# A decoder layer on one core: the chunk tails in seven steps fewer, with the knots counted at once and the picks transposed a step sooner

## What is computed

```python
x = x + attn(layernorm(x))            # softmax over 1024 keys, 16 heads
x = x + xattn(layernorm(x), ctx, mask)
# routed part, on xf = layernorm(x):
def _calibrate(scores, knots, temperature):        # 8 knots
    idx_float = sigmoid(scores / (temperature[0] + 1e-6)) * (K - 1)
    idx_low = clip(int(idx_float), 0, K - 2)
    t = idx_float - idx_low
    return knots[idx_low] + t * (knots[idx_low + 1] - knots[idx_low])
cluster_idx = argmax(_calibrate(xf @ cluster_sigs.T))     # 8 clusters
local_idx = argmax(_calibrate(xf @ sigs.T)[of that cluster])  # 8 tiles in each
comp = tanh(gelu(xf @ w1 + b1) @ w2 + b2)
mag = relu(comp . spline_w1[tile] + b) . spline_w2[tile] + b
y = xf + mag * directions[tile] * output_scale
x = x + layernorm(y) * gamma + beta
```

## Time and profile before

| | us |
|---|---|
| median of 3 runs | 1819.47 |
| lowest, highest | 1817.64, 1820.15 |
| the profiled execution's own time | 1818.39 |
| its span, first to last instruction | 1816.1 |
| PE busy | 1727.1 |
| DVE busy | 1163.6 |
| ACT busy | 1143.8 |
| POOL busy | 892.8 |

### The profile page before, as it was taken

One profiled execution on the slowest core, in us unless ns is written; L12 is line 12 of the kernel. 1 busy time (PEld: TensorE's weight loads), 2 busy tenths in 40 slices (PEclk: granted clock), 3 DMA queues, 4 the chain that ended last, 5 costly groups with the idle time before them and its releaser, 6 DMA issues.

```text
span 1816.1 us, 27480 instructions
## 1 busy us (share of the span) xinstructions
PE 1727.1 (95%) x9160; PEld 831.3 (46%) x9160; DVE 1163.6 (64%) x2784; ACT 1143.8 (63%) x1554; POOL 892.8 (49%) x811
## 2 busy tenths in 40 slices
PE   6999999999999899999999999999999999999994
PEld 4444454454544344454444435445454444544352
DVE  6575538567476765747657576665756767385767
ACT  5577756666476765666566764676656677567652
POOL 2444454645544544546645364545645456444620
PEclk9999999999999999999999999999999999999997
DMA  4300000101200000010200000001020001000000
GB/s 146 74 13 1 1 13 1 36 1 24 48 1 13 1 24 1 1 36 1 58 13 1 13 1 24 1 1 36 1 59 1 2 1 24 13 1 1 1 12 12
DMA packets 97246, 32.39 MB, mean 18 GB/s; under 512 B 76753, under 2 KB 91217, under 8 KB 97105
## 3 DMA queue, kind: packets, MB, share of 16 engines
q1 hardware_dynamic: 97104, 30.64, 8.1%
HBM read 13.56 MB, written 4.19 MB: 10 GB/s over the span
## 4 chain that ended last, share of the span: by engine, by line
PE 79%; ACT 8%; DVE 7%; issue 4%; POOL 1%; DMA 0%; ACTq 0%; DVEq 0%; SPq 0%; POOLq 0%
PE attended L1387 22%; PE key_scores L1366 21%; PE misc L1295 7%; PE misc L1427 6%; PE max_scores L1344 6%; PE misc L1467 3%; PE misc L1397 3%; ACT relu L1770 2%; ACT probs L1779 2%; PE misc L1458 2%; PE misc L1531 1%; PE misc L1300 1%; DVE relu L2073 1%; PE misc L1520 1%; PE misc L1509 1%
## 5 line engine op out<-in xcount | busy, mean ns | idle before, releaser
L1779 ACT ACTIVATE probs<-key_scores 128x1024 f32<-128x1024 f32 x512 | 524.6, 1025 | 455.9 <-PE key_scores L1366 392.7
L2581 POOL TENSOR_TENSOR prob_sum<-prob_sum,probs 128x512 f32<-128x512 f32 x383 | 492.2, 1285 | 133.0 <-ACT probs L1779 108.8
L1387 PE MATMUL attended<-probs,values 128*64 128x512 f32 x2048 | 551.4, 617 | 0.1
L2073 DVE CUSTOM_DVE_ANT_0 relu<-max_scores,relu 128x512 f32<-128x512 f32 x508 | 330.2, 687 | 248.5 <-PE max_scores L1344 247.1
L1366 PE MATMUL key_scores<-q_high,k_chain 64*128 64x512 f32 x2048 | 457.9, 443 | 19.0 <-ACT probs L1779 17.5
L1366 PEld LDWEIGHTS key_scores<-q_high,k_chain 64*128 64x128 f32 x2048 | 191.6, 184 | 459.2 <-ACT probs L1779 226.8
L2095 DVE TENSOR_TENSOR running_sum<-running_sum,probs 128x512 f32<-128x512 f32 x384 | 266.3, 694 | 11.4 <-ACT probs L1779 4.3
L1770 ACT ACTIVATE relu<-max_scores 128x1024 f32<-128x1024 f32 x254 | 259.1, 1020 | 13.5 <-PE max_scores L1344 10.8
L2577 POOL TENSOR_TENSOR prob_sum<-probs 128x512 f32<-128x512 f32 x64 | 82.1, 1283 | 349.2 <-PE misc L1397 342.3
L1344 PE MATMUL max_scores<-k_max,q_high 64*128 64x512 f32 x1016 | 209.6, 408 | 11.9 <-DVE row_max L2073 10.7
L1366 PE MATMUL key_scores<-q_low,k_chain 64*128 64x512 f32 x1024 | 202.9, 392 | 0.0
(11 more groups left out here) (457 smaller groups left out, 1897.4 us busy)
## 6 DMA issues: line engine op xcount, KB each, us to landing
k_chain<-k_chain SPq DMA_DIRECT2D x32, 256.0 KB, 3.7
shift_row<-row_max SPq DMA_DIRECT2D x512, 0.5 KB, 2.0
buf_a<-in_x SPq DMA_DIRECT2D x8, 512.0 KB, 4.0
x_in<-in_x SPq DMA_DIRECT2D x7, 512.0 KB, 4.8
k_max<-k_max SPq DMA_DIRECT2D x14, 256.0 KB, 3.5
out_x<-buf_b SPq DMA_DIRECT2D x7, 512.0 KB, 3.2
heads_out<-in_qkv_wT SPq DMA_DIRECT2D x1, 1536.0 KB, 10.0
wo<-in_o_wT SPq DMA_DIRECT2D x1, 1024.0 KB, 6.3
```

Of the source, the lines that this page charges most:

```text
L1387: tensor.matmul(attended[head * HD:(head + 1) * HD, :], values_of(b, g // 2)[:, kt, g % 2 * HD:(g % 2 + 1) * HD], prob_slot(u, kt, head), ...
L1779: scalar.activation(probs[(u * KT + kt) % len(probs)][:, :, :], key_scores[:, :, :], ACT.Exp).then_inc(S["exp"])
L2073: vector.tensor_tensor_reduce(out=relu_of(u, i)[:, head, :], in0=max_area(u, i)[:, head, :], in1=relu_of(u, i)[:, head, :], scale=1.0, sca ...
L2581: gpsimd.tensor_tensor(prob_sum[1][:, :], prob_sum[1][:, :], probabilities, ALU.add).then_inc(S["prob_sum1"])
```

## The change

In `calibration` one yield goes: `cal_d` and `cal_e` now stand in the same step as `cal_b`. In `tail` one yield before `pickT` goes, so that the transposition is put in the step after `pick_one`; `mag` loses its own step and is put in the same step as the first `y`; the second `gamma` and the first `x3` share a step. As `calibration` is run twice, seven yields go in each tail. In `attention` ROOM pieces may be put in every step from step 501 on. No instruction is added or taken away.

```diff
@@ calibration
     plan.put("cal_b", j, which)
-    yield LATE
     plan.put("cal_d", j, which)
     plan.put("cal_e", j, which)
@@ tail
     plan.put("pick_one", j)
-    yield LATE
     yield EARLY
     plan.put_in_bank("pickT", j)
@@
     plan.put("spline", j)
-    yield LATE
-    plan.put("mag", j)
     yield BOTH
     for pair in range(nt // 2):
         plan.put_in_both_banks("directions", (j, pair), [("y", "y", j, pair)] * 2)
         yield LATE if pair else ROOM
+        if not pair:
+            plan.put("mag", j)
         plan.put("y", j, pair)
@@
     plan.put("root", j)
-    for pair in range(nt // 2):
-        yield LATE
-        plan.put("gamma", j, pair)
-    for pair in range(nt // 2):
-        yield LATE
-        plan.put("x3", j, pair)
+    yield LATE
+    plan.put("gamma", j, 0)
+    yield LATE
+    plan.put("gamma", j, 1)
+    plan.put("x3", j, 0)
+    yield LATE
+    plan.put("x3", j, 1)
     plan.put("store", j)
@@ attention
-        room = (step + MAX_AHEAD) % 2 == 0
+        room = (step + MAX_AHEAD) % 2 == 0 or step + MAX_AHEAD >= UNITS * KT
```

## The result

| | before | after |
|---|---|---|
| median, us | 1819.6 (4 runs) | 1896.1 (4 runs) |
| lowest, highest | 1817.6, 1820.2 | 1892.6, 1896.2 |
| the profiled execution's own time | 1818.4 | 1896.0 |
| its span | 1816.1 | 1894.2 |
| PE busy | 1727.1 | 1759.1 |

The ratio is 1.042 (95% interval 1.040 to 1.044). I had forecast 1843 with a range up to 1860: the direction was right, the size was off by 53 us.

A forecast was written before the change was run, and what follows sets the result against it. PE bounds the kernel (79% of the chain), so waits that lengthen score steps count. Tail terms summed to 21.6 us, plus 2 for the clock: 1818.4 became 1842 profiled, 1843 median, range 1828 to 1860.

The forecast's parts named there:

- The clock: Half TensorE speed behind new waits: one fall counted among some six new waits over 1.6 us, +2 us.
- rival (a): The clock falls behind nearly every new wait: 15 waits at 1.7, up to 24 us more, 1860 to 1867; chance 10%.
- work that only moves: Fewer lane steps, `gamma` and `x3` joined, `store` ending earlier: 0, with 0.5 us either way in all.
- stretched instructions: Small DVE instructions lengthened beside POOL's: taken as 0, one in each chain, about 6 us, kept for the upper end.
- The wait for the first `y`: `mag` before `y`, PE waiting at second `directions`: -0.8 in tails 0 to 4, +0.7 in 5, +1.7 and +0.6 in 6.
- `pickT`: PE reaches it before `pick_one` ends: +1.3 in tails 0, 2, 4, +2.0 in 5 and 6, +0.45 in 1 and 3.
- picked clusters: `pick_tiles` and `tile_scores` before the maxima's reduction: -0.2 in tails 5 and 6, 0 in 0, 2, 4, +1.9 in 1, 3.
- first calibration: `cal_g` late before the maxima's reduction: +1.35 in tails 0, 2, 4, +1.1 in 1 and 3, -0.2 in 5 and 6.
- second calibration: `cal_g` behind POOL delays the next maxima's reduction: +1.85 in tails 5 and 6, 0 in 0, 2, 4, +0.5 in 1, 3.
- What I said would show it: Timeline signs: maxima waits over 20 us, `pickT` over 1 us in five tails, second `directions` waiting in tails 5 and 6 only.

The follow-up runs named there:

- `fill_pick`: Changed kernel plus unused filler matmuls before TensorE's wait at `pickT`, three in tails 0, 2 and 4, six in the others: 1890.3 us.
- `apart`: Kernel before, with the second `directions` of tails 0 to 4 one step later: 1813.8 us against 1819.3 (ratio 0.9971).
- `apart_tiles`: `apart` with `tile_scores` one step later and the second calibration's exponential one more in tails 1, 3 and 5: 1810.7 us against 1819.4 (0.9953).

## Why the prediction was right in sign and 53 us short

**The clock, 30 us.** I took 2 us, one fall. PE's busy time grew by 32.0. The price of a fall was sized about right (up to 1.7; 1.5 to 1.6 measured). The number of falls failed: I set one against some six new waits, from one fall in two looks. There were 15 stretches. The rival (a) named this mechanism with 15 waits and 24 us, and I gave it 10%. What I had missed is that the waits' number was itself too low: 27 waits of PE over 1.2 us stand in the changed kernel at the maxima, at `pickT` and for `y`, where before there were two.

**`gamma` and `x3`, 15 us.** I put 0 with 0.5 either way for "work that only moves". In tails 0 to 4 the joined pair came to stand at kt 2 and 3, behind `sums`, where POOL sums and divides back to back. It cost 0.66 and 2.30 of idle time in each, 14.8 in all, and none in tails 5 and 6, where the pair stands at kt 0 and 1. The failed step: I looked for waiters of the moved work and not for what runs on POOL in its new steps. The stretched instructions stood in my text as one in each chain, 6 us as the upper end. My text also allowed "one or two" of them in a tail, "inside the 6"; two would have been 0.9 x 14, some 13 us.

**The wait for the first `y`, 9 us.** I gave -1.0 over all tails. It was +4.0 at the second `directions` and +4.1 at `x_prep`'s transposition. Where I wrote "0.7 to 0.8 of wait is left", 1.3 was left in tails 0, 2 and 4 (1.2 before, so nothing was gained), and 2.0 to 2.2 in tails 5 and 6. In tails 1 and 3 the second `directions` are free of a wait, as I said, and the 0.8 is gone. But `x_prep` wants the same bank two steps sooner, and I had not looked at who else takes the banks (PE, changed kernel, tail 1):

```profile
649.84 0.63 PE L1299 MATMUL misc<-consts_sb,x_in 128*128 128x128 f32 x4 [2.04 <-DVE buf_b L2476]
```

The size failed too. I had the end of `y` 3.8 after the reduction begins (3.7 in tail 2, 3.95 in tail 5), but counted PE's arrival, 2.9 to 3.1, from the step's begin, which in tail 2 is 0.55 earlier; in tail 5 PE was there 2.0 after the reduction began. Tail 5 shows the case with next to nothing stretched (0.48 for 0.22 in one instruction): two reductions, the sum, `mag` and `y` against `attended` and scores of PE (DVE and PE, changed kernel).

```profile
1571.02 0.48 DVE L2461 SCALAR_TENSOR_TENSOR buf_c<-buf_c,small 128x64 f32<-128x64 f32 x1
...
1572.25 0.88 DVE L2476 SCALAR_TENSOR_TENSOR buf_b<-misc,mag,buf_b 128x256 f32<-128x256 f32 x2
...
1573.18 1.23 PE L1605 MATMUL misc<-direction_table,p2T 64*128 64x256 f32 x4 [2.01 <-DVE buf_b L2476]
```

**`pickT`, 3 us.** 8.8 forecast, 11.9 measured: 1.7 to 1.9 for 1.3 in tails 0, 2 and 4, 2.5 for 2.0 in tails 5 and 6, 1.4 for 0.9 in tails 1 and 3 together.

**The calibrations and the picked clusters were right in sum, and that by luck.** The waits of the maxima grew by 27.7; less 14.8 of `gamma` and `x3` that is 12.9, and my terms for both calibrations and the picked clusters were 21.6 - 8.8 + 1.0 = 13.8. Inside the sum the errors cancel. In tail 2 the first calibration showed 0.31 + 1.17 where I had 1.35, and the second cost 0.2 to 0.6 in tails 0, 2 and 4 where I had 0. In tails 1 and 3 the three terms cost 2.9 and 2.2 where I had 3.5, in tail 5 2.7 and in tail 6 1.1 where I had 1.45. In tail 6 PE ran at half clock between the two waits, so it came later to the second, which is 0.55 there and 2.09 in tail 5.

The four terms make 57 us more than forecast; 0.9 for the calibrations and 1.7 for `x_prep`'s own input go off. That leaves the 54 by which the profiled execution missed (1896.0 for 1842), 53 in the medians.

**What I said would show it.** Shown: the maxima's waits on `row_max` over 20 us (38.4), `pickT`'s wait on POOL over 1 us in five tails (0.95 and 0.47 in the other two), waits at the second `directions` in tails 5 and 6 and none in tails 1 and 3. Shown in tail 5 alone: PE's wait over 1.5 at the maxima behind `cal_g` of the second calibration (2.09; 0.55 in tail 6), and the exponential that waits there for POOL's sum (2.60; step 495 of tail 6 waited for PE's scores).

Settled by runs are the price of `mag`'s two instructions, and that `gamma` and `x3` cost by their place and their joining together. The 30 us of the clock rest on PE's busy time with an equal count of matmuls, tail by tail, and on `fill_pick` for the price of one stretch. The waits at `x_prep` are read from the trace, and no run took them out alone. What decides which wait brings the fall was not settled.

## What to carry to other kernels

A piece moved to another step meets other neighbours: read not only who waits for it but who else wants its banks, and what the engine that shares its memory port does there, for even an instruction of four elements can last as long as the other engine's largest. Don't cost an edit's parts as a sum when each shifts the ones behind it; put the new steps of all pieces beside the busy stretches first. Where waits come close together, count the half clock behind each at about half its length before trusting a sum of waits; and where a wait is for work that is only a step too close, one step more is worth more than several steps fewer.

## What the runs showed of the hardware that I had not expected

- A DVE instruction of 128x4 elements lasted 0.99 and 1.31 us beside POOL's 128x512 sums and 0.17 and 0.23 us alone, and ended to within 0.03 us with POOL's current instruction. The two in this chain cost about one POOL instruction each. The Trainium skill (SBUF — State Buffer, section "Who interferes with whom") says that the shared ports are held for a whole instruction and that the other engine blocks; the trace agrees. I had cited that rule for `mag` and not drawn the sum from it.
- The half clock came behind waits as short as 1.17 us (PE idle in step 239 of `fill_pick`) when others stood near, and the same wait had none in tail 2 of the changed kernel: 7.00 against 5.50 us for the step.
- The half-clock time doesn't follow the sum of the waits. `apart` has 6.7 us less idle time of PE from step 64 on than the kernel before and 10 us at half clock, where the kernel before had 3.4; `apart_tiles` has 3.4 again.
